# Half-head rounds in the first attention, with the maxima of two key chunks on the two halves of the array's rows

## The reference

```python
qkv = x @ Wqkv.T + bqkv
qkv = qkv.reshape(B, H, S, 3 * hd)          # reshaped without a transpose
q, k, v = jnp.split(qkv, 3, axis=-1)
scores = jnp.einsum('bhsd,bhtd->bhst', q, k) * (1.0 / math.sqrt(hd))
attn = jax.nn.softmax(scores, axis=-1)
vals = jnp.einsum('bhst,bhtd->bhsd', attn, v)
vals = vals.reshape(B, S, D)
return vals @ Wo.T + bo
```

## Time and profile before

| stage or engine | from the profile |
|---|---|
| median of three runs | 3471.16 us |
| span of the profiled execution | 3463.3 us |
| TensorE, VectorE, ScalarE, GpSimd busy | 3092.5, 2371.1, 1441.1, 811.3 us |
| projection begins (first matmul of line 251) | 19.08 us |
| first max matmul | 75.46 us |
| first scores | 117.6 us |
| last division of L0 (line 444) starts | 954.91 us |

### The profile page before, as it was taken

The page is one execution under the profiler, slowest core; times in us unless marked ns, Lnnn a source line. Parts: engine busy times, 40 slices in busy tenths (PEclk is TensorE's granted clock), DMA queues, the critical chain, the costliest instruction groups (busy, mean ns, idle before and its releaser), DMA issues. The chain is left out here.

```text
span 3463.3 us, 39811 instructions
## 1 busy us (share of the span) xinstructions
PE 3092.5 (89%) x14168; PEld 1729.6 (50%) x14168; DVE 2371.1 (68%) x4742; ACT 1441.1 (42%) x2519; POOL 811.3 (23%) x623
## 2 busy tenths in 40 slices
PE   5999999999978999999999999999997575566799
PEld 3444444444354555555555555555544243444576
DVE  5877777877327777777777777777745667665553
ACT  0466666666721444444444444443442203000343
POOL 2000000000002444344444444434440000444100
PEclk6799999999986999999999999999998676555698
DMA  3011011010013111101111111111100000000100
GB/s 79 3 13 13 7 13 13 7 13 7 1 44 74 37 29 33 29 21 37 37 37 37 37 37 25 32 24 31 37 1 12 0 7 2 1 1 3 29 1 13
DMA packets 35834, 76.13 MB, mean 22 GB/s; under 512 B 5926, under 2 KB 27356, under 8 KB 28636
## 3 DMA queue, kind: packets, MB, share of 16 engines
q1 hardware_dynamic: 35636, 73.59, 10.4%
HBM read 17.74 MB, written 5.24 MB: 7 GB/s over the span
## 5 line engine op out<-in xcount | busy, mean ns | idle before, releaser
L875 ACT ACTIVATE l1a_PT<-l1a_st 128x512 f32<-128x512 f32 x1024 | 604.9, 598 | 874.8 <-PE l1a_st L784 867.8
L892 DVE TENSOR_REDUCE l1a_m<-l1a_aux 128x1 f32<-128x512 f32 x1024 | 673.4, 686 | 185.7 <-PE l1a_aux L747 170.5
L429 DVE TENSOR_REDUCE l0s_m<-l0s_mx 128x1 f32<-128x512 f32 x1024 | 634.8, 683 | 203.2 <-PE l0s_mx L351 203.2
L843 POOL TENSOR_TENSOR l1a_acc<-l1a_acc,l1a_PT 128x1024 f32<-128x1024 f32 x224 | 555.6, 2480 | 716.0 <-ACT l1a_PT L875 716.0
L414 ACT ACTIVATE l0s_PT<-l0s_st 128x512 f32<-128x512 f32 x1024 | 554.7, 601 | 325.7 <-PE l0s_st L369 320.0
L797 PE MATMUL l1a_ov<-l1a_PT,l1a_V 128*64 128x512 f32 x2048 | 510.1, 620 | 0.0
L351 PE MATMUL l0s_mx<-l0a_KS,l0a_QS 96*128 96x512 f32 x1024 | 447.2, 462 | 11.5 <-DMA l0a_KS<-qk_parts 11.5
L782 PE MATMUL l1a_st<-l1a_QA,l1a_KA 128*128 128x512 f32 x1024 | 451.2, 441 | 2.3 <-issue 2.3
L784 PE MATMUL l1a_st<-l1a_QB,l1a_KB 65*128 65x512 f32 x1024 | 413.7, 404 | 0.0
L369 PE MATMUL l0s_st<-l0a_QS,l0a_KS 97*128 97x512 f32 x1024 | 402.7, 408 | 10.9 <-ACT l0s_PT L414 8.7
L747 PE MATMUL l1a_aux<-l1a_KA,l1a_QA 128*128 128x512 f32 x1024 | 404.6, 437 | 7.1 <-DMA l1a_QA<-l1a_lo 5.5
(11 more groups left out here) (350 smaller groups left out, 3105.4 us busy)
## 6 DMA issues: line engine op xcount, KB each, us to landing
l1a_KA<-l1a_hi SPq DMA_DIRECT2D x32, 512.0 KB, 7.9
l1a_QA<-l1a_hi SPq DMA_DIRECT2D x16, 512.0 KB, 4.6
l1a_QA<-l1a_lo SPq DMA_DIRECT2D x16, 512.0 KB, 4.1
l1a_QB<-l1a_hi SPq DMA_DIRECT2D x16, 512.0 KB, 4.6
l1a_KB<-l1a_lo SPq DMA_DIRECT2D x16, 512.0 KB, 6.5
l0a_QS<-qk_parts SPq DMA_DIRECT2D x64, 64.0 KB
l0a_KS<-qk_parts SPq DMA_DIRECT2D x64, 64.0 KB
l3f_w<-in_L_ffn_w SPq DMA_DIRECT2D x3, 792.0 KB
```

The costliest lines, as they stand in the source:

```text
L429: nc.vector.tensor_reduce(m4[:, h % 2, q, c:c + 1], src, axis=AX.X, op=ALU.max).then_inc(mx_read, 1)
L843: nc.gpsimd.tensor_tensor(acc[:, h % 2, 1, :], first, PT[:, g % PT_SLOTS, :], ALU.add).then_inc(added_pool, 1)
L875: nc.scalar.activation(PT[:, g % PT_SLOTS, (u % 2) * CW:(u % 2 + 1) * CW], st[:, u % ST1, :], ACT.Exp).then_inc(exp_done, 1)
L892: nc.vector.tensor_reduce(m4[:, b, q, c:c + 1], src, axis=AX.X, op=ALU.max).then_inc(aux_read, 1)
```

## The change: what it does

- The work goes by units of half a head (1024 queries), 32 in all, and rounds of four scores, four max tasks and one set of values, 8 rounds for a unit, 256 in all. Score matmuls of two key tiles and two query chunks make a round.
- QS and KS hold the operands in four copies of 24 rows (q hi, lo, hi against k hi, hi, lo), each at the start of a strip of 32 rows, with the scale divided by 4. The scores use all 128 rows. A max matmul uses 56 rows (two copies and the gap), at row 0 for the even key chunks and at row 64 for the odd ones. Row 120 of QS takes the maxima, and KS holds -2 there.
- The maxima of a unit are reduced straight into `mrow` (line 453 of the new kernel) with the queries taken in a stride of 8, and placed without the transpose.
- There are 4 banks `mx` with a semaphore each. A reduction (line 446) increments `reduced`, VectorE waits for it, and increments `mx_free` of the bank by itself.
- The scores trail the max tasks by LEAD0 = 10 rounds. The last 10 rounds have no max tasks.
- The projection is no stage of its own. Its matmuls are tasks of the same plan (DENSE0): chunk 0 ahead of all, the rest between the first rounds. ScalarE fills q, k and V; VectorE takes the rest `lo` (four of 1024 columns). q and k go to DRAM (`qk_rows`) by six DMAs of 64 KB for a head (`place`), and back by eight of 24 rows (192 KB) for a head (`load`).
- QS and KS are set in `load_stage`, by VectorE and ScalarE.
- `ov` is one bank, copied out once for a unit (32 times); the transposes are four matmuls against a 32-column selection matrix, with two VectorE instructions as before, each on half as much.
- GpSimd clears the stage's semaphores in `token_major_out`.

```diff
+        @block.scalar
+        def _(act):
+            act.wait_ge(ident_zero, 2)
+            nc.scalar.activation(KS[:, :, :], ones[:, 0:1].unsqueeze(2).broadcast_to([P, BUF0, S]), ACT.Copy,
+                                 scale=M_SCALE0)
+
+        @block.vector
+        def _(dve):
+            nc.vector.memset(QS[:, :, :].bitcast(F32), 0.0)
...
+GR0 = 4
+R0 = 3 * HD0
+KMX0 = 2 * 32 - HD0
+MROW0 = 3 * 32 + R0
+HALF0 = S // 2
+TILES0 = HALF0 // P
+UNITS0 = 2 * H0
+ROUNDS0 = TILES0
+LEAD0 = ROUNDS0 + 2
+BUF0, MX0, ST0, PT0 = 3, 4, 3, 6
+LOADS0 = 2 * GR0
+M_SCALE0 = -2.0
+DENSE0 = {-4: [("v", 0)], -2: [("qk", 2), ("qk", 3)], -1: [("qk", 4), ("qk", 5)], 0: [("qk", 6)], 1: [("qk", 7)],
+          2: [("v", 1)], 3: [("v", 2)], 4: [("v", 3)]}
...
-                if slot[key] >= MX0:
-                    pe.wait_ge(mx_read, slot[key] - MX0 + 1)
...
-                if kind == "max":
-                    q, c = divmod(i, NC)
-                    last = nc.tensor.matmul(o, QS[0:KR0, h % 3, q, :], KS[0:KR0, h % 3, TPC * c:TPC * (c + 1), :],
+                kind, i = key
+                n = slot[key]
+                if n >= MX0:
+                    pe.wait_ge(mx_free[n % MX0], n // MX0)
+                o = mx[:, n % MX0, :]
...
+                elif kind == "max":
+                    n, c = divmod(i, NC)
+                    u, tile = divmod(n, TILES0)
+                    h, half = divmod(u, 2)
+                    if i % (2 * GR0 * TILES0) == 0:
+                        pe.wait_ge(heads_in[h % BUF0], 16 * LOADS0 * (h // BUF0 + 1))
+                    r = slice(64 * (c % 2), 64 * (c % 2) + KMX0)
+                    q = QS[r, h % BUF0, half * HALF0:(half + 1) * HALF0].rearrange("r (k i) -> r i k", i=TILES0)
+                    last = nc.tensor.matmul(o, q[:, tile, :], KS[r, h % BUF0, c * CW:(c + 1) * CW],
                                             start=True, stop=True)
...
+                for e in range(2):
+                    for qc in range(2):
+                        col = 32 * (2 * qc + e)
+                        last = nc.tensor.matmul(ov[col:col + 32, :], V[:, u // 2, 2 * n + e, :],
+                                                PT[:, (2 * r + e) % PT0, qc, :], start=(n == 0),
+                                                stop=(n == ROUNDS0 - 1), skip_group_check=True)
...
+            for g in range(END):
+                tasks, r = plan[g + 1], g - LEAD0
+                if 0 <= r < ALL:
+                    scores(4 * r)
+                    scores(4 * r + 1)
+                for key in tasks[:2]:
                     mx_task(key)
-                if g < H0 * STEPS:
-                    scores(2 * g + 1)
-                if g % 2 and LAG0 <= g < H0 * STEPS + LAG0:
-                    values((g - LAG0) // 2)
-                for key in tasks[some:]:
+                if 0 <= r < ALL:
+                    scores(4 * r + 2)
+                    scores(4 * r + 3)
+                if 1 <= r < ALL + 1:
+                    values(r - 1)
+                for key in tasks[2:]:
                     mx_task(key)
...
                 if kind == "max":
-                    q, c = divmod(i, NC)
-                    nc.vector.tensor_reduce(m4[:, h % 2, q, c:c + 1], src, axis=AX.X, op=ALU.max).then_inc(mx_read, 1)
-                    if i == NMX - 1:
-                        dve.wait_ge(mx_read, n + 1)
-                        nc.vector.tensor_reduce(mneg[:, h % 2, :], m4[:, h % 2, :, :], axis=AX.X, op=ALU.max,
-                                                negate=True).then_inc(m_done, 1)
...
+                    r, g = divmod(i, NC)
+                    u, tile = divmod(r, TILES0)
+                    dve.wait_ge(mx_full, n + 1)
+                    nc.vector.tensor_reduce(mquad[:, u % 2, tile, g:g + 1], mx[:, n % MX0, :],
+                                            axis=AX.X, op=ALU.max).then_inc(reduced, 1)
+                    dve.wait_ge(reduced, i + 1)
+                    dve.sem_inc(mx_free[n % MX0], 1)
+                    if i % (GR0 * TILES0) == GR0 * TILES0 - 1:
+                        if u >= 2:
+                            dve.wait_ge(m_placed[u % 2], 16 * (u // 2))
+                        nc.vector.tensor_reduce(mrow[:, u % 2, :], mquad[:, u % 2, :, :], axis=AX.X,
+                                                op=ALU.max).then_inc(m_done, 1)
+                    if i % GR0 == GR0 - 1 and r - LEAD0 in (-1, 0, 2):
+                        split_low((1, 2, None, 3)[r - LEAD0 + 1])
...
+                    nc.vector.reciprocal(r, o[:, :, :, HD0]).then_inc(rden_done, 1)
+                    dve.wait_ge(rden_done, i + 1)
+                    nc.vector.tensor_tensor(
+                        vals[:, h, half * 64:(half + 1) * 64].rearrange("p (q j c) -> p j q c", q=2, c=HD0),
+                        o[:, :, :, 0:HD0], r.unsqueeze(3).broadcast_to([P, TPC, 2, HD0]), ALU.mult
+                    ).then_inc(mx_free[n % MX0], 1)
...
+            def place(h):
+                sp.wait_ge(split, h // TPC + 1)
+                for i, copies in enumerate(((hi, lo, hi), (hi, hi, lo))):
+                    for n, part in enumerate(copies):
+                        sp.dma_start(rows[i, h, n * HD0:(n + 1) * HD0, :, :].rearrange("c j p -> j c p"),
+                                     part[:, i, h * P:(h + 1) * P].bitcast(F32)).then_inc(rows_out[h % 4], 16)
+
             def load(h):
-                if h >= 3:
-                    sp.wait_ge(pv_done, J0 * (h - 2))
-                for dst, rows in ((QS, (0, 1, 0, 1)), (KS, (2, 2, 3, 3))):
-                    for r, part in enumerate(rows):
-                        sp.dma_start(dst[r * HD0:(r + 1) * HD0, h % 3, :, :].bitcast(F32),
-                                     parts[part, :, h * P:(h + 1) * P].rearrange("(j c) p -> c j p", c=HD0)
-                                     ).then_inc(parts_in[h % 3], 16)
-
...
+                sp.wait_ge(rows_out[h % 4], 16 * 6 * (h // 4 + 1))
+                if h >= BUF0:
+                    sp.wait_ge(st_full, 8 * ROUNDS0 * (h - BUF0 + 1))
+                for g in range(GR0):
+                    r = slice(32 * g, 32 * g + R0)
+                    sp.dma_start(QS[r, h % BUF0, :].rearrange("r (j p) -> r j p", p=P).bitcast(F32),
+                                 rows[0, h, :, :, :]).then_inc(heads_in[h % BUF0], 16)
+                    sp.dma_start(KS[r, h % BUF0, :].rearrange("r (j p) -> r j p", p=P).bitcast(F32),
+                                 rows[1, h, :, :, :]).then_inc(heads_in[h % BUF0], 16)
+
+            place(0)
+            load(0)
...
+                if half == 0 and u >= 2 and h + 2 < H0:
                     load(h + 2)
...
+                    if h + 3 < H0:
+                        place(h + 3)
```

More of the change, by code:

```diff
@@ L416, in _ @@
-                if n == 2 and h >= 1:
-                    copy_out(h - 1)
-            copy_out(H0 - 1)
+                for b in (2 * g, 2 * g + 1):
+                    act.wait_ge(st_full, b + 1)
+                    nc.scalar.activation(PT[:, g % PT0, b % 2, :], st[:, b % ST0, :], ACT.Exp).then_inc(exp_done, 1)
+                if g % 2:
+                    fills(g // 2)
+                u, n = divmod(g, 2 * ROUNDS0)
+                if n == 1 and u >= 1:
+                    copy_out(u - 1)
@@ L472, in token_major_out @@
+            for i in range(2):
+                sp.wait_ge(m_placed[i], 16 * (UNITS0 // 2))
+    return used
+def token_major_out(nc, ctx, tag, W, w_dram, b_dram, vals, X, ident, ones, used):
     sb, ps, sem = stage_memory(nc, ctx, tag)
```

351 lines of the change are left out of this document (167 added, 184 removed).

## The result

The changed kernel takes 3519.72 us (median of 4 runs, 3516.88 to 3525.42); the kernel before took 3472.14 in the same comparison. The ratio is 1.0132, with a 95% interval of 1.0119 to 1.0146: 47.6 us slower, where the prediction said 20. The direction and VectorE's price came as predicted; the size did not: 3519.72 lies above the forecast's own range of 3475 to 3512, and TensorE, not VectorE, sets the pace.

What follows compares the result with a forecast made beforehand. VectorE was to bound the kernel at 3.42 us a round, TensorE 3.41, taken as 3.45. Stage: 81 + 849 + 12 + 27 + 4 = 973, about 975, 20 us more; forecast 3491 us, own range 3475 to 3512, 8 in 10 within 3450 to 3570.

Steps and rivals of the forecast that it cites:

- VectorE's price: Max reductions: waiting for each and incrementing mx_free separately makes one cost 0.83 us, where it was 0.60.
- The first rival: VectorE isn't held by the separate increment: 2.49 us a round, TensorE sets the pace; 3389 to 3472, middle 3430; chance 0.14.
- VectorE bound: Attention rounds: VectorE sets the pace at 3.42 to 3.5 us a round; range 3475 to 3512 us, chance 0.54.
- the prediction's own sign: Attention stage: the prediction is wrong if VectorE waits for TensorE in most rounds, or the stage ends before 950.
- TensorE's pair P: Two max matmuls on the two row halves: 0.14 + 0.33 = 0.47 us, twice a round; bounds 0.30 and 0.67.
- within the upper bound: Strided queries as weights, in no row: their cost was to lie within the pair's 0.67 us, TensorE's 3.81 a round.
- Behind the start: First rounds after scores begin: V's three other tasks and the half clock cost 12 us, about 9 and 3.
- the second rival: The pairs don't run together: a pair costs 0.67, TensorE 3.81 a round, 89 us more, 3580; chance 0.17.
- Start, lead, end and loads: First max matmul at 40 us, scores at 81; ten last rounds 27 us plus 4; 1.5 MB loaded in 7.5 us.
- the maxima were not late: Rival: the odd unit's placing on SyncE stands behind loads and writes at 62 GB/s, giving 3560 us; chance 0.07.
- The step from span to median: Whole kernel: 7.9 us added to the predicted span of 3483.3, as the median stands above it, giving 3491.
- The pairing saves nothing against 3.05: TensorE's round of 3.41 us against 3.05 before: extra changes of array use take what running together gives.

Runs made afterwards that it cites:

- the two kernels that it bounds: The changed kernel with max-matmul queries as 128 neighbouring columns, 3490.40 us; the changed kernel with all maxima on rows 0 to 119 of the whole array, 3484.38 us.

## Why the prediction was wrong

- **VectorE's price was right.** 0.83 predicted, 0.84 in the lead and wherever VectorE sets the pace, and 0.60 with the hand-back by the reduction. Its round was right too: 3.42 predicted, 3.41 in the two kernels that it bounds. The first rival (not held) is out. But VectorE does not bound the changed kernel, so the forecast's central claim, "VectorE bound", was wrong by the prediction's own sign.
- **The step that failed is TensorE's pair P.** It was put at 0.47 (0.14 for a second load of weights behind the first, 0.33 to the next use) and measured 0.56. The working was wrong in both parts: the two loads of a pair run at once, and the cost is one whole load and 0.25. With contiguous queries that is 0.43, below the 0.47; with the strided ones it is 0.56. The prediction saw the stride, had no row for it, and left it "within the upper bound" while the middle of the range took no account of it. Twice 0.09 lifts TensorE from 3.41 to 3.59 (3.548 measured, since the rest of the round came 0.04 cheaper: 2.32 for 2.34, and 0.11 for the selection's 0.13), over VectorE's 3.42. The sum was built on two engines that were equal to within 0.01; an error upwards in either went straight into the round. 240 rounds times 0.098 is the 23 us.
- **Behind the start, 12 was too little.** V's three tasks were put at 9 us of time and the half clock at 3, taken as it rose once. But it had risen before the scores began, and fell behind the first V task. Measured: 42.8 - 6 x 3.548 = 21.5. Three kernels take it apart. Without V tasks the first six rounds take 26.4, 5 us over six average rounds, for which the prediction had no term. With them at a clock of 1.00 they take 36.2, so the tasks cost 9.8, and the 9 was right. The last 6.6 are the clock, put at 3.
- **The pairs run together**, which refutes the second rival. That rival's price was too low as well: it took a pair at 0.67 and the round, selection included, at 3.81. With both on one half a pair is 0.80 and the eight rounds of a unit take 32.2, 4.03 each (3.91 for a plain one), and the kernel takes 3660.57 where the rival had 3580.
- **Start, lead, end and loads were right** to 2 us each; the maxima were not late.
- **The step from span to median** took 7.9 for what lies around the span. It is 1.8. The other 6.1 were the distance of that one execution from its median. To add the 20 to the median was sound all the same, for another reason than given.
- "The pairing saves nothing against 3.05", in the prediction, was right, and too mild: against a whole-array kernel the halves lose 0.05 us a round (3.19 against 3.14) with contiguous queries, and 0.16 (3.44 against 3.28) with strided ones. The two kernels that differ in nothing else, the ones with the transpose and the spread V tasks, are 22 us apart.

On the Trainium skill's rule that a semaphore after each instruction costs nothing extra (VectorE: DVE Perf Modes, The DRAIN you can't avoid), the runs show both sides: a reduction that increments by itself costs nothing, 0.60 us apart; a wait for its own end and an increment by VectorE cost 0.24 more. On the rule that matmuls on different row groups start about 4 ns apart (TensorE: Matmul & The Clock Gate, Part 3), the trace agrees as to the matmuls (0.63 us for two that last 0.62 each). But P did not become its lower bound of 0.30: it is 0.56, and 0.43 with the short loads, since the loads ahead of the matmuls count.

## What to carry to other kernels

Where two engines come out equal in the sum, look for the one term without a row and work the round out with its worst value too: the larger sum decides. Weights read in small steps cost time here wherever no running matmul hid the load: behind the values, and at each pair on the halves. Before splitting the array, count the loads that lie bare and what the neighbours lose. Here two maxima in sequence on the whole array take 0.47 to 0.57 and two at once on halves 0.43, but the scores between them take 0.47 in the first case and 0.66 in the second. And a fully busy TensorE does not show that it sets the pace: look at who waits, and take away one bound at a time.
